# VectorE makes the fourth normalised tile, the second q and k projections move from chunks 5 and 6 to 9 and 10, and the expert counts spread over three slots

## What is computed

```
xn  = layernorm(x)                               # no gain, no bias
a   = layernorm(xn) * ln1_g + ln1_b              # a second norm of the normalised rows
Q, K, V = a projected by low-rank weights, 16 heads of 8
attn = softmax(causal(Q K^T / sqrt(8)));  ctx = attn V
h   = xn + ctx out_U out_V
att = h + gelu(layernorm(h) fc1) fc2             # low-rank MLP

logits = xn @ Wr                                 # 9 experts
p = softmax(logits); best two, weights made to sum to 1
ffn = sum over the two: w_e * (silu(xn Wg_e) * (xn Wu_e)) Wd_e

out = x + att + ffn
```

## Time and profile before

| | us |
|---|---|
| median of 3 runs | 1020.24 (1019.96 to 1023.8) |
| the profiled execution | 1026.66 |
| span of its trace | 1024.9 |

### The profile page before, as it was taken

The page is one execution under the profiler, slowest core; times in us unless marked ns, Lnnn a source line. Parts: engine busy times, 40 slices in busy tenths (PEclk is TensorE's granted clock), DMA queues, the critical chain, the costliest instruction groups (busy, mean ns, idle before and its releaser), DMA issues. The chain is left out here.

```text
span 1024.9 us, 25256 instructions
## 1 busy us (share of the span) xinstructions
PE 966.5 (94%) x7701; PEld 751.0 (73%) x7701; DVE 697.8 (68%) x3179; ACT 539.5 (53%) x1256; POOL 428.5 (42%) x563
## 2 busy tenths in 40 slices
PE   4788999999999999999999969999999999999997
PEld 3456566666666666666666639999999999998896
DVE  5649689777777777777777844455555554558887
ACT  1662355555555555555555655555555555564442
POOL 9461122245454454445545413445444444440100
PEclk9766899999999999999999988999999999999999
DMA  9384363354554464434433214222222222238784
GB/s 238 117 235 158 146 217 128 102 148 130 136 154 119 126 165 129 125 106 124 126 110 114 72 46 116 57 68 62 64 66 63 64 66 61 73 117 234 209 233 134
DMA packets 135109, 127.12 MB, mean 124 GB/s; under 512 B 17290, under 2 KB 115716, under 8 KB 134980
## 3 DMA queue, kind: packets, MB, share of 16 engines
q1 hardware_dynamic: 111248, 67.76, 24.5%
q0 software_dynamic: 20592, 56.43, 17.7%
q10 hardware_dynamic: 3140, 1.33, 0.5%
HBM read 57.15 MB, written 42.60 MB: 97 GB/s over the span
## 5 line engine op out<-in xcount | busy, mean ns | idle before, releaser
L1413 DVE CUSTOM_DVE_ANT_0 att_masked_st<-att_m_ps,att_mask_st 128x128 bf16<-128x128 f32 (+1 forms) x1024 | 311.1, 353 | 108.4 <-PE att_m_ps L1015 65.0
L829 ACT ACTIVATE att_probs<-att_t_ps 128x512 f32<-128x512 f32 x384 | 229.3, 598 | 211.8 <-PE att_t_ps L1039 195.9
L1663 POOL DMA_INDIRECT y_scratch<-moe_y,moe_row_now x136 | 132.2, 972 | 155.6 <-DVE moe_y L1917 97.6
L650 POOL DMA_INDIRECT slot_x<-att_xs,att_slot_now x128 | 126.9, 991 | 165.0 <-PE att_t_ps L1039 140.0
L1911 DVE TENSOR_TENSOR moe_hidden<-moe_gate,moe_up_ps 128x352 f32<-128x352 f32 x136 | 70.9, 521 | 109.9 <-issue 80.0
L1039 PE MATMUL att_t_ps<-att_mask_ts,att_ident_b 128*128 128x256 bf16 (+1 forms) x384 | 124.1, 323 | 0.0
L1740 PE MATMUL moe_y_ps<-w_down,moe_hidden_t 128*128 (+1 forms) x816 | 114.3, 276 | 3.3 <-ACT moe_hidden_t L1847 2.2
L1838 ACT ACTIVATE moe_gate<-moe_gate_ps 128x352 f32<-128x352 f32 x136 | 63.2, 465 | 96.1 <-PE moe_up_ps L1723 96.1
L1740 PEld LDWEIGHTS moe_y_ps<-w_down,moe_hidden_t 128*128 128x128 f32 (+1 forms) x816 | 101.8, 191 | 5.6 <-issue 5.4
L1413 DVE DVE_READ_ACCUMULATOR2_ANT att_row_max<- 128x1 f32 x1024 | 84.9, 83 | 0.0
L1038 PE MATMUL att_t_ps<-att_odd_stack,att_k_stack 97*128 97x512 f32 x192 | 81.4, 424 | 3.1 <-DMA att_odd_stack<-att_neg_max 2.7
(11 more groups left out here) (262 smaller groups left out, 2060.3 us busy)
## 6 DMA issues: line engine op xcount, KB each, us to landing
att_k_stack<-att_qk_parts POOLq DMA_DIRECT2D x96, 128.0 KB
slot_x<-att_xs POOLq DMA_DIRECT2D x17, 516.0 KB, 3.1
moe_x<-slot_x SPq DMA_DIRECT2D x34, 258.0 KB
att_xs<-xn_scratch SPq DMA_DIRECT2D x32, 256.0 KB
mlp_rows<-y_scratch POOLq DMA_DIRECT2D x16, 512.0 KB, 5.7
even_stack<-att_qk_parts SPq DMA_DIRECT2D x192, 32.0 KB
att_odd_stack<-att_qk_parts SPq DMA_DIRECT2D x192, 32.0 KB
xn_scratch<-first_words POOLq DMA_DIRECT2D x16, 256.0 KB, 3.6
```

Source lines behind the costliest of these rows:

```text
L650: pool.indirect_dma_start(env["slot_x"][:], bass.IndirectOffsetOnAxis(ap=slot_now[c.parity][:, col:col + 1], axis=0), xs[c.parity][:, t, k ...
L829: act.activation(probs[:, m % PT, :], t_ps[m % 2][:], ACT.Exp).then_inc(exp_done, 1)
L1413: last = dve.tensor_tensor_reduce(out=masked_st[m % 2][:, part], in0=m_ps[m % 2][:, part], in1=mask_st[:, SEQ - width:], scale=1.0, scalar ...
L1663: pool.indirect_dma_start(env["y_dram"][:], bass.IndirectOffsetOnAxis(ap=row_now[q.parity][:, t:t + 1], axis=0), y[c.parity][:], None).the ...
```

## The change

It has four parts.

1. x is loaded in six loads (8, 8, 16, 16, 8, 8 tiles).
2. The fourth tile of `xnr` is made by DVE, ahead of its four tiles of xn, straight from x by `both_rstd`. POOL keeps the stores and the stacks of k. DVE makes three chunks first (before: four) and is then three chunks ahead of its `copy_logits`.
3. Chunk 1's q and k are projected in rounds 9 and 10 (before: 5 and 6). POOL's stack of chunk 1's k follows the store of chunk 14 (before: of chunk 10).
4. `count_tiles` runs in slots 7, 8 and 9, three experts each, `count_all` and the first `count_half` in slot 11, the second in slot 13, all in bank `pv_ps[1]`, which `probs_times_v` first writes in slot 15. The wait for DVE's copies moves from the projection in slot 14 to there. DVE's links of slots 7, 8, 10, 12 and 14 move to 9, 10, 12, 14 and 15.

```diff
-        X_PARTS = (16, 16, 16, 8, 8)
+        X_PARTS = (8, 8, 16, 16, 8, 8)
...
-        Q_AT, K_AT, V_AT = (1, 5), (2, 6), 4
+        Q_AT, K_AT, V_AT = (1, 9), (2, 10), 4
         LATE_FOLD = (3, 5, 7)
+        COUNT_AT = (7, 8, 9)
...
-                pool.wait_ge(ln_ready, 2)
+                pool.wait_ge(ln_ready, 1)
                 for c in range(chunks):
                     store_xn(c)
-                    if c >= XB:
-                        pool.wait_ge(xt_turned, c - XB + 1)
-                    tile = c * TPC + TPC - 1
-                    pool.tensor_scalar(xnr[c % XB][:, TPC - 1, :], x_all[:, tile, :], rstd2[:, tile:tile + 1], None, ALU.mult).then_inc(xnr_pool, 1)
...
                 def turn(c):
                     pe.wait_ge(xnr_act, c + 1)
-                    pe.wait_ge(xnr_pool, c + 1)
+                    pe.wait_ge(xnr_dve, c + 1)
...
+                    if u == 0 and seq == 1:
+                        pe.wait_ge(half_copied, 2)
...
-                        if slot == 6 and first:
-                            count_tiles(0)
-                        if slot == 9 and first:
-                            count_all(0)
-                            count_half(0, 0)
+                        if slot in COUNT_AT and first:
+                            count_tiles(range(EXPERTS)[COUNT_AT.index(slot)::len(COUNT_AT)])
                         if slot == 11 and first:
-                            count_half(0, 1)
+                            count_all()
+                            count_half(0)
+                        if slot == 13 and first:
+                            count_half(1)
...
                 def normalise_x(c):
+                    if c >= XB:
+                        dve.wait_ge(xt_turned, c - XB + 1)
+                    tile = c * TPC + TPC - 1
+                    dve.tensor_scalar(xnr[c % XB][:, TPC - 1, :], x_all[:, tile, :], mean[:, tile:tile + 1], both_rstd[:, tile:tile + 1],
+                                      ALU.subtract, ALU.mult).then_inc(xnr_dve, 1)
                     for t in range(TPC):
...
                 normalise_x(2)
-                normalise_x(3)
                 for c in range(chunks):
-                    if c + 4 < chunks:
-                        normalise_x(c + 4)
+                    if c + 3 < chunks:
+                        normalise_x(c + 3)
```

More of the change, by code:

```diff
@@ L878, in _ @@
                 act.wait_ge(logits_copied, chunks)
-                act.wait_ge(xnr_pool, chunks)
+                act.wait_ge(xnr_dve, chunks)
                 for k in range(XB):
@@ L978, in count_half @@
                         pe.wait_ge(half_copied, 1)
-                    pe.matmul(free_ps[bank][:, to], earlier_of, chosen.rearrange("p t e -> p (t e)")[:, part], start=True, stop=False)
-                    pe.matmul(free_ps[bank][:, to], ones[0:tiles, :], earlier.rearrange("k t e -> k (t e)")[:, part],
+                    pe.matmul(pv_ps[1][:, to], earlier_of, chosen.rearrange("p t e -> p (t e)")[:, part], start=True, stop=False)
+                    pe.matmul(pv_ps[1][:, to], ones[0:tiles, :], earlier.rearrange("k t e -> k (t e)")[:, part],
                               start=False, stop=True).then_inc(counted, 1)
@@ L1279, in routing_links @@
                     dve.wait_ge(logits_copied, chunks)
-                    dve.wait_ge(xnr_pool, chunks)
+                    dve.wait_ge(xnr_dve, chunks)
                     dve.wait_ge(xn_stored, 16 * chunks)
@@ L1305, in routing_links @@
                     yield
[L1306 to L1307 removed]
+                    dve.wait_ge(tile_counted, len(COUNT_AT))
+                    dve.tensor_copy(tile_count, pv_ps[1][0:tiles, 0:EXPERTS]).then_inc(count_copied, 1)
                     yield
```

29 lines of the change are left out of this document (13 added, 16 removed).

## The result

The changed kernel takes 1026.69 us (median of 7 runs, 1023.82 to 1028.09), the kernel before 1020.99 (7 runs): a ratio of 1.0044, 95% interval 1.0027 to 1.0061. The change costs 5.7 us by the medians (4.5 us by the ratio, with 2.8 to 6.2 inside its interval), where 6.5 us of gain were forecast, and the time lies 6 us above the range's upper end. The profiled execution took 1027.6 us, with a span of 1025.7.

The account below looks back on a forecast made before the run. Attention was taken as bound by TensorE and 80 to 100 us by VectorE, the first stage by a loop of waits. Gains of 4.1 (first stage) + 2.4 (counts) = 6.5 us off 1020.24 gave 1013.7 us, range 1009.8 to 1020.6.

Parts of the forecast that it names:

- What bounds the kernel: Attention from 120 us is bound by TensorE; whatever is won or lost before passes to the end one for one.
- Part 1: Start of the kernel, x in six loads: 0 us, +-0.3, as VectorE limits the last 32 statistics.
- Parts 2 and 3 up to chunk 7: First stage: waits for POOL go, chunk 7's logits at about 58.8 in place of 64.18, lead 5.4 us.
- The walk behind chunk 7: First stage, from chunk 7's logits at 58.8 to the end at 76.3 in place of 80.44: 4.1 us won.
- the ring: First stage, rounds 9 to 12: VectorE, ACT's three tiles, turn, score and score back close every 2.4 us.
- The clock in the first stage: At the second fold: full clock kept by the skill's rule, 4.1 us won; if it falls, 1.8 (0 to 2.5).
- case C: The counts keep the full clock, the first stage doesn't: 1.8 + 2.4 us won, 1016.0 us; chance 0.21.
- Rival D: First stage: POOL waits were hidden anyway, longer queues eat the rest; 1.8 + 0.3 or less won, about 1018.5; chance 0.12.
- Part 4: Attention step 0, counts moved: 0.8 + 2.5 (clock) - 0.9 = 2.4 us won; without the clock 0.3.
- B: The first stage keeps the full clock, the counts don't: 4.1 + 0.3 us won, 1015.8 us; chance 0.18.
- Rival E: First stage: VectorE becomes the bound at the half clock; 3.8 us lost with the counts, 1024.0 us; chance 0.09.

Follow-up runs that it names:

- e3: The kernel before, not edited, measured again as the control: ratio 1.0013 to the kernel before.
- e2: The changed kernel with the counts as before, so parts 1 to 3 of the change alone: ratio 1.0011 to the kernel before.
- e15: e12 with POOL's second stack of k behind the store of chunk 11 in place of chunk 7: ratio 0.9930 to the kernel before.
- e10: The changed kernel with VectorE four chunks ahead of the logits in place of three: ratio 0.9999 to the kernel before.
- e1: The kernel before with part 4 of the change alone, counts in slots 7, 8 and 9: ratio 1.0035 to the kernel before.
- e5: The changed kernel with all nine counts in slot 7 in place of three each in slots 7 to 9: ratio 0.9999 to the kernel before.
- e8: The kernel before with parts 2 and 3 of the change alone, five loads and counts as before: ratio 1.0007 to the kernel before.
- e4: The changed kernel with the five loads of before, so part 1 undone: ratio 1.0036 to the kernel before.
- e6: The changed kernel with each count 32 columns wide in place of one, still in slots 7 to 9: ratio 1.0017 to the kernel before.
- e11: The changed kernel with nine counts of 32 columns, all in slot 7: ratio 1.0002 to the kernel before.
- e12: The changed kernel with five loads, VectorE four chunks ahead and nine counts of 32 columns in slot 7: ratio 0.9965 to the kernel before.

## Why the prediction was wrong

**What bounds the kernel** was right: through attention, from slot 16 on, the kernel only shifts (the changed one is 3.8 us behind the first trace of before at step 1, and 4.1 at step 15; 7.0 and 5.7 behind e3's). Single traces don't keep that distance to the end. From the start of the last exponential of attention to the end, the first trace of before needs 421.8 us, e3's 417.2 and the changed one 418.4, so that the spans are only 0.8 us apart in the first pair and 6.9 in the second. This is also what the prediction had wrong where it set aside, as "nothing here", that its profiled execution lay 6.4 us above the median: the second trace of the same kernel has chunk 7's logits 2.3 us sooner and chunk 15's at 78.16.

**Part 1**, 0 +-0.3: right as far as it can be told. The last 32 statistics still take 6.29 us in one run; they began at 18.98 in place of 18.44, inside the scatter of the start.

**Parts 2 and 3 up to chunk 7** were right to a tenth in the place: the waits for POOL are gone, 58.85 against 58.8. The lead that goes with it, 5.4, was read from one late trace; by the means (63.0 in the four traces with the first stage of before, 58.7 in the five with all of parts 1 to 3) it is 4.3.

**The walk behind chunk 7** is the first step that failed: 4.1 us won in the text; on average 1.1 lost in the traces (chunk 15's logits at 80.4 in the mean of the five kernels with all of parts 1 to 3 unaltered, at 79.3 in that of the four with the first stage of before), and a ratio of 1.0011 for e2. I gave rounds 7 to 10 7.8 us (three rounds of 2.35 and one lower half), and they took 10.6: the stores of xt and the stacks. I had called SP no bound by its issue time, 1.85 us a round, and had not looked at how long a transfer takes to land once the DMA engines are full, though the earlier trace rows shows a share of 1.02 already before the change. The prediction named this as what would make it wrong; in e15's trace the waits shrink once POOL's second stack of k is moved. Rounds 10 to 15 took 11.1 where I had 9.7: the step "as xn is made only three chunks ahead, the ring [...] closes every 2.4 us as well" was taken for a detail of the same size as VectorE's own round. It is the price of the change: VectorE makes the tiles of a chunk one round later than before, and the last of them (73.92 to 75.03) is followed by ACT's three tiles, a turn and a score before chunk 13's logits, which wait 2.43 us. e10 gives 3.2 us back by making one chunk more ahead, some 0.9 of them through the clock.

**The clock in the first stage** was half right. It fell at 58.5 us and stayed down for 10.2, as in case C, and fell again at 75.6; but with it at half, VectorE wasn't the bound either, it waited. The sum for this case doesn't come out of its own terms: 4.1 less 2.2 for the ring and 1.05 for one projection is 0.9 us won, not 1.8. Rival D had half of what happened, "if VectorE, with xn one chunk less ahead, is what turns wait for, one releaser is only replaced by another", and still counted 1.8 us as won; the transfers stood in none of the rivals.

**Part 4** is the step that cost the time, and its sign was wrong: +2.4 forecast, -3.6 measured (e1's ratio, 1.9 to 5.2 by its interval). Slot 6's unit did come free of the counts, at 103.89 where 103.45 was forecast. But the gap ahead of it only changed its releaser: 1.13 us for VectorE's unit, where there had been 1.37 for its link, and the clock fell behind it as before (106.3 against 105.8). With the half clock as short as before the part is worth 1.1 to 1.8 us, above the 0.3 that was taken without the clock (slots 6 to 16: 21.0 in e5, whose counts stand in one slot, against 22.1 in both traces of before and 22.7 and 22.9 in e2 and e8). What failed is "Since the fall of the clock at about 106 came right behind this gap and the one-column passes, it may go". I took the gap for the likelier cause, and for the passes noted under B only that they "still have next to no columns"; I never asked whether three groups could be worse than one. The half clock grew from 6.8 to 17.1 us, and against e5, with 6.8 us of it and otherwise the same work, slots 6 to 16 take 5.4 us more (26.5 against 21.0): half a us for every us of half clock. Against e4, with 3.4 us of it and the same order of work in these slots, it is 0.4. The 2.5 us that I had hoped to win were reckoned at 0.3/0.8 of it.

The Trainium skill (TensorE: Matmul & The Clock Gate, HAM oscillation) ties the drop to idle gaps between matmuls, and by that rule less waiting means a full clock. The trace of e1 agrees as far as the fall goes, which came behind a wait of 1.12 us, and disagrees on what follows, with PE busy 2.00 of 2.00 us in each stretch at 0.50. The measurement decides.

**Rival E** had the right side and the wrong mechanism: slower, but through the counts and the ring of the look-ahead, not through VectorE at the half clock.

What stays open: why nine narrow passes in three groups tend to hold the clock down and in one group less, why e4's trace with the same three groups had only 3.4 us of it, and what separates e6's two kinds of runs; no run here separates the passes' columns from their weight loads, or their spread from the moment at which the clock falls.

## What to carry to other kernels

Keep passes with almost no columns together in one piece; spread over a busy stretch they can cost more through the clock than they hide. Judge this by many runs, as one trace can show the opposite. When work moves to an engine that has slack on average, check how far ahead of its consumer it still runs in the last rounds, where there is no slack. And a lead won in a loop is only as good as the next queue: look at how full the DMA engines are and move transfers wanted late out of the microseconds in which others are wanted soon. Judge them by the time that others then take to land, not by their bytes.

## What the runs showed of the hardware

Counts of 1 and of 32 columns cost nearly the same, 2.32 and 2.35 us for nine (e5, e11), and those of 1 column as much at the full clock as at half (six passes 0.88 us at 105.22 with the clock at 1.00, and 0.88 at 110.86 at 0.50).

The scatter of one kernel's times goes in part with its clock: over the 35 runs of before beside e1 to e4, the five at a mean granted clock of 0.972 average 1021.0 us and the one at 0.963 takes 1025.7, but the six at 0.970 lie between 1018.0 and 1024.5; e6 shows 1016.8 at 0.973 and 1030.9 at 0.959. Two traces of the kernel before have spans of 1024.9 and 1018.8 us.

A DMA share near 1.0 says nothing of the bytes: 180 GB/s were moved at 1.04 (e12) and 317 at 0.96 (e15).
